# Mixer weight split in the first stage, h_in biases moved, second expert's low part inside slot 0

## The reference

```python
h = tok_embedding(x) * 16                     # tables of 256, 64, 16 and 4 columns, each projected to 256
n = layernorm(h)
x1 = n @ w1.T + w1_b
x_conv = silu(depthwise_conv3(x1))            # along the 128 positions
x_ssm = ssm(x_conv)                           # linear recurrence over positions, 16 states a channel
v = silu(n @ v1.T + v1_b)
h = h + (x_ssm * v) @ w2.T + w2_b             # the "mixer"
n = layernorm(h)
shared = (silu(n @ sw1 + sb1) * (n @ sw3 + sb3)) @ sw2 + sb2      # 512 hidden
out = (expert_a(n) + expert_b(n)) / 2         # 2 of 8 experts, each gelu(n @ w1 + b1) @ w2 + b2, 256 hidden
h = h + (shared + out) / 2
```

## Time and profile before

| | |
|---|---|
| median of three runs | 444.79 us (443.84 to 445.13) |
| profiled execution: its own time | 444.33 us |
| profiled execution: its span | 442.4 us, 8454 instructions |
| PE busy | 399.5 us (90%) |
| PEld (weight loads, beside PE) | 350.9 us (79%) |
| DVE busy | 281.8 us (64%) |
| ACT busy | 242.5 us (55%) |
| POOL busy | 213.1 us (48%) |

### The profile page before, as it was taken

The page is one execution under the profiler, slowest core; times in us unless marked ns, Lnnn a source line. Parts: engine busy times, 40 slices in busy tenths (PEclk is TensorE's granted clock), DMA queues, the critical chain, the costliest instruction groups (busy, mean ns, idle before and its releaser), DMA issues.

```text
span 442.4 us, 8454 instructions
## 1 busy us (share of the span) xinstructions
PE 399.5 (90%) x2880; PEld 350.9 (79%) x2880; DVE 281.8 (64%) x608; ACT 242.5 (55%) x435; POOL 213.1 (48%) x235
## 2 busy tenths in 40 slices
PE   3878899899998864799999999999999999998996
PEld 2767788888678762598898998988988988887885
DVE  6668998989655779866556465565554554655333
ACT  4675778778886335544544645635635635535442
POOL 7769998821008256547446337247247237333000
PEclk9999999999998989799999999999999999999999
DMA  2442121259799972100121021111201301100101
GB/s 63 122 148 95 43 66 52 73 166 305 220 309 282 254 273 84 50 0 3 54 90 46 31 68 48 53 42 47 80 15 48 92 3 48 47 0 0 49 0 47
DMA packets 32779, 38.86 MB, mean 88 GB/s; under 512 B 3461, under 2 KB 29027, under 8 KB 32624
## 3 DMA queue, kind: packets, MB, share of 16 engines
q1 hardware_dynamic: 29616, 32.99, 24.6%
...
...
## 4 chain that ended last, share of the span: by engine, by line
PE 67%; DVE 17%; ACT 6%; issue 4%; DMA 3%; POOL 1%; DVEq 0%; ACTq 0%; POOLq 0%; SPq 0%
PE ps L1139 20%; PE ps L1140 20%; PE ps L1141 20%; DVE hid_lo L1070 3%; DMA toep_l<-kernel_rows_dram 2%; DVE stat L948 2%; PE ps L1222 2%; PE ps L1177 2%; PE ps L1258 1%; DVE h2n L961 1%; DVE sw_lo L1017 1%; PE ps L1147 1%; DVE catT_lo L941 1%; DVE act_out L1064 1%; DVE hnT L990 1%
## 5 line engine op out<-in xcount | busy, mean ns | idle before, releaser
L1070 DVE SCALAR_TENSOR_TENSOR hid_lo<-act_out,hid_hi 128x512 fp32r<-128x512 f32 x64 | 56.2, 879 | 56.6 <-ACT hid_hi L855 56.6
L842 ACT ACTIVATE act_out<-ps,vec 128x512 f32<-128x512 f32 x32 | 22.1, 689 | 91.4 <-PE ps L1141 91.4
L1064 DVE SCALAR_TENSOR_TENSOR act_out<-ps,vec,act_out 128x512 f32<-128x512 f32 x32 | 24.0, 750 | 53.4 <-ACT act_out L842 53.4
L667 POOL TENSOR_TENSOR h_sb<-h_sb,bias_e 128x256 f32<-128x256 f32 x32 | 24.4, 766 | 53.4 <-DVE h2n L961 53.4
L1140 PE MATMUL ps<-h2nT_lo,sw_hi 128*128 128x512 f32 x128 | 50.0, 391 | 0.0
L1141 PE MATMUL ps<-h2nT_hi,sw_lo 128*128 128x512 f32 x128 | 50.0, 391 | 0.0
L1139 PE MATMUL ps<-h2nT_hi,sw_hi 128*128 128x512 f32 x128 | 49.9, 390 | 0.0
L660 POOL TENSOR_TENSOR zc_lo<-v_sb,zc_hi 128x256 fp32r<-128x256 f32 x32 | 29.6, 924 | 34.9 <-ACT zc_hi L832 34.9
L846 ACT ACTIVATE act_out<-ps,vec 128x512 f32<-128x512 f32 x32 | 22.1, 689 | 41.1 <-PE ps L1141 41.0
L527 POOL DMA_INDIRECT cat<-table_dram,x_ids x32 | 36.4, 1139 | 8.2 <-issue 5.8
L855 ACT ACTIVATE hid_hi<-act_out 128x512 fp32r<-128x512 f32 x64 | 39.7, 622 | 0.0
...
## 6 DMA issues: line engine op xcount, KB each, us to landing
...
```

Source lines behind the costliest of these rows:

```text
L667: nc.gpsimd.tensor_tensor(at, at, bias_e[:, bass.ds(e, 1), :].rearrange("p o c -> p (o c)"), ALU.add).then_inc(h2_biased, 1)
L842: nc.scalar.activation(act_out[:, n % 4, :], ps[bank][:, :], ACT.Silu, bias=vec[:, C_SB1 + j:C_SB1 + j + 1]).then_inc(act_done, 1)
L1064: nc.vector.scalar_tensor_tensor(act_out[:, n % 4, :], ps[bank + 1][:, :], vec[:, C_SB3 + j:C_SB3 + j + 1], act_out[:, n % 4, :], ALU.add, ...
L1070: nc.vector.scalar_tensor_tensor(hid_lo[:, n % 4, :], act_out[:, n % 4, :], 0.5 if kind == SHARED else 0.25, f32(hid_hi[:, n % 4, :]), ALU ...
```

## The change

Piece 0 gets a raw buffer of its own in the free end of `flat` (Toeplitz slot 3). It is loaded behind the first h store, cast by ScalarE behind the last hn of group 0, and its low part is formed by GpSimd at the start of the last group; SyncE waits for that low part before it loads Toeplitz slot 3. ScalarE's and VectorE's instructions for it between the recurrence and the mixer are gone, as are SyncE's load there and its wait ahead of piece 7. GpSimd adds the bias to both h_in buffers before piece_lo(1), and piece_lo(8) moves from ahead of slot 0 into mixer_1, behind its second mixer_bias.

```diff
--- before.py
+++ after.py
@@ -109,6 +109,7 @@
     power = flat[:, 0:HALVES * STATES * SEQ].rearrange("p (s t) -> p s t", t=SEQ)
     raw_at = HALVES * STATES * SEQ
     raw_a = flat[:, raw_at:raw_at + (KC + 4) * D]
+    raw_w2 = flat[:, raw_at + (KC + 5) * D:raw_at + (KC + 7) * D]
     k_sum = flat[:, raw_at + (KC + 4) * D:raw_at + (KC + 5) * D].rearrange("p (h t) -> p h t", t=SEQ)
 
 
@@ -387,13 +388,13 @@
 
 
     free = o_sb[:, :, :, :].rearrange("p a g c -> p (a g c)")
-    raws = [stage[:, 0, :], stage[:, 2:4, :], stage[:, 1, :]] + [free[:, n * BLK:(n + 1) * BLK] for n in range(4)]
+    raws = [raw_w2, stage[:, 2:4, :], stage[:, 1, :]] + [free[:, n * BLK:(n + 1) * BLK] for n in range(4)]
     raws += [stage[:, 0, :], stage[:, 2:4, :]]
     his = [w2_hi[:, :, :].rearrange("p k n -> p (k n)"), ex1_hi[:, :, :]] + [sw_hi[:, n, :] for n in range(6)]
     los = [w2_lo[:, :, :].rearrange("p k n -> p (k n)"), ex1_lo[:, :, :]] + [sw_lo[:, n, :] for n in range(6)]
     his, los = his + [ex0_hi[:, :, :]], los + [ex0_lo[:, :, :]]
     sources = [w_b[:, 0, :], w_e[RES - 1]] + [w_b[:, n, :] for n in range(1, 7)] + [w_e[0]]
-    LO_BY = (0, 1, 0, 0, 0, 0, 0, 0, 1)
+    LO_BY = (1, 1, 0, 0, 0, 0, 0, 0, 1)
     PIECES = [(raws[n], his[n], los[n], piece_sem[n], 16, LO_BY[n], LO_BY[:n + 1].count(LO_BY[n]), sources[n])
               for n in range(9)]
 
@@ -428,10 +429,15 @@
             toep_part(q, 0, HALF if q >= TRING else 0)
             toep_part(q, 1, 0)
 
+        def piece_in(n):
+            raw, _, _, signal, _, _, _, src = PIECES[n]
+            sp.dma_start(raw, src).then_inc(signal, 16)
+
         for r in range(RES):
             h_store(0, r)
             if r == 0:
                 sp.dma_start(raw_a[:, KC * D:], w_a[:, KC * D:]).then_inc(wa_in, 16)
+                piece_in(0)
         sp.dma_start(bias_row[:, 0:1, :], bass.AP(rows.tensor, D, [[0, P], [D, 1], [1, D]])).then_inc(rows_in, 16)
         sp.dma_start(bias_e[:, :, :], bass.AP(rows.tensor, 2 * D, [[0, P], [D, RES], [1, D]])).then_inc(rows_in, 16)
         with sp.Fori(1, GROUPS - 1) as i:
@@ -442,6 +448,8 @@
             if r == 1:
                 sp.wait_ge(k_out, 16)
                 sp.wait_ge(wv_lo_done, 2)
+            if r == 1 + TRIGHT:
+                sp.wait_ge(w_lo_done[1], 1)
             if 2 <= r < 2 + TRIGHT:
                 toep_load(r - 2)
 
@@ -464,10 +472,6 @@
             sp.dma_start(dst[bass.ds(r, 1), :, :, :].rearrange("o p g c -> (o p) g c"),
                          o_sb[:, par, :, :]).then_inc(stored[par], 16)
 
-        def piece_in(n):
-            raw, _, _, signal, _, _, _, src = PIECES[n]
-            sp.dma_start(raw, src).then_inc(signal, 16)
-
         def piece_used(n):
             sp.wait_ge(w_lo_done[PIECES[n][5]], PIECES[n][6])
 
@@ -476,15 +480,12 @@
         h_load(0, 0)
         sp.wait_ge(bias_step, BIAS_STEPS)
         sp.dma_start(w2_bias, bass.AP(rows.tensor, 0, [[0, P], [D, 1], [1, D]])).then_inc(rows_in, 16)
-        piece_in(0)
         piece_in(1)
         h_load(1, 1)
         piece_in(2)
         sp.wait_ge(ssm_done, 2 * NQ)
-        for n in range(3, 7):
+        for n in range(3, 8):
             piece_in(n)
-        piece_used(0)
-        piece_in(7)
         piece_used(1)
         piece_in(8)
         sp.wait_ge(h2_done, GROUPS)
@@ -590,9 +591,16 @@
                 pool.dma_start(kernel_rows, k_row[:, :, :, :].rearrange("p n c w -> p (n c w)").bitcast(F32)
                                ).then_inc(k_out, 16)
 
+        def piece_lo(n):
+            src, hi, lo, _, _, _, _, _ = PIECES[n]
+            pool.wait_ge(w_hi_done, n + 1)
+            nc.gpsimd.tensor_tensor(lo, src, f32(hi), ALU.subtract).then_inc(w_lo_done[1], 1)
+
         def group(i):
 
             for r in range(RES):
+                if i == GROUPS - 1 and r == 0:
+                    piece_lo(0)
                 if r % 2 == 0 and (r or i):
                     power_pair(RES * i + r - 2, (r - 2) % 4)
                 if r + LEAD < RES:
@@ -672,6 +680,7 @@
             for g in range(2):
                 mixer_lo(1, g)
                 mixer_bias(0, 0, g)
+            piece_lo(8)
             for g in range(GROUPS):
                 power_step(GROUPS + g, g, eps2_done, rstd2_done)
                 if g < 2:
@@ -710,20 +719,14 @@
             need(pool, l2_done, UNITS * e + 2, half_set)
             expert_split(e + 2, par, times)
 
-        def piece_lo(n):
-            src, hi, lo, _, _, _, _, _ = PIECES[n]
-            pool.wait_ge(w_hi_done, n + 1)
-            nc.gpsimd.tensor_tensor(lo, src, f32(hi), ALU.subtract).then_inc(w_lo_done[1], 1)
-
         pool.wait_ge(rows_in, 48)
         add_w2_bias(0, 1)
+        add_w2_bias(1, 1)
         piece_lo(1)
         for g in range(GROUPS):
             mixer_lo(0, g)
         for g in range(GROUPS):
             power_step(g, g, eps2_done, rstd2_done)
-        add_w2_bias(1, 1)
-        piece_lo(8)
         pool.wait_ge(w_lo_done[0], LO_BY.count(0))
         expert_in(2, 0)
         slot(0, 0, 2)
@@ -742,6 +745,11 @@
         nc.scalar.activation(warm_out[:, 0:1], zero[:, :], ACT.Silu)
         act.wait_ge(wa_in, 16)
         nc.scalar.copy(proj_hi[:, :, :].rearrange("p k n -> p (k n)"), raw_a[:, 0:KC * D]).then_inc(wa_hi, 1)
+
+        def piece_hi(n):
+            src, hi, _, signal, count, _, _, _ = PIECES[n]
+            act.wait_ge(signal, count)
+            nc.scalar.copy(hi, src).then_inc(w_hi_done, 1)
 
         def cat_hi(i, r):
             n = RES * i + r
@@ -767,6 +775,8 @@
             need(act, hn_turned, r // 2 - 1)
             nc.scalar.activation(hn[:, r % 4, :], h_ring[:, r % 4, :], ACT.Identity, bias=shift[:, r % 4:r % 4 + 1],
                                  scale=rstd[:, r % 4:r % 4 + 1]).then_inc(hn_first, 1)
+            if r == 7:
+                piece_hi(0)
             if r == 5:
                 act.wait_ge(wa_in, 32)
                 nc.scalar.copy(wv_hi[:, :, :, :].rearrange("p a k n -> p (a k n)"), raw_a[:, KC * D:]).then_inc(wa_hi, 1)
@@ -805,12 +815,6 @@
         act.wait_ge(pad_zero, 1)
         run_phase_a(act, {"cat": cat_hi, "emb": h_out, "norm": norm, "hn": hn_hi, "x": x_hi_part, "out": out_, "silu": silu})
 
-        def piece_hi(n):
-            src, hi, _, signal, count, _, _, _ = PIECES[n]
-            act.wait_ge(signal, count)
-            nc.scalar.copy(hi, src).then_inc(w_hi_done, 1)
-
-
         for q in range(NQ):
             if q == 1:
                 act.wait_ge(rows_in, 32)
@@ -820,7 +824,6 @@
             for bank in range(2):
                 act.wait_ge(ssm_done, 2 * q + bank + 1)
                 nc.scalar.copy(y_at(q, bank), y_part(q, bank, 1)).then_inc(y_low, 1)
-        piece_hi(0)
         act.wait_ge(ssm_done, 2 * NQ)
         piece_hi(1)
 
@@ -1102,8 +1105,6 @@
 
         for u in range(8, 16):
             z_part(u)
-            if u == 9:
-                piece_lo(0)
         for g in range(GROUPS):
             mixer_out(0, 0, g)
             if g >= 1:
@@ -1331,7 +1332,7 @@
         pe.wait_ge(y_done, 2 * NQ)
         for u in range(8, 16):
             y_turn(u)
-        pe.wait_ge(w_lo_done[0], 1)
+        pe.wait_ge(w_lo_done[1], 1)
         for g in range(GROUPS):
             mixer_mm(0, g)
         for g in range(GROUPS):
```

## The result

The changed kernel takes 441.38 us (median of 4 runs, 441.22 to 442.19) where the kernel before took 444.60 (443.84 to 445.13) beside it: ratio 0.9928, 95% interval 0.9904 to 0.9952. The forecast was 441.5.

The account below looks back on a forecast made before the run. The bound was when the near-continuous matmul stream from mixer_mm(1,0) starts, set by VectorE's sw_lo, GpSimd's DMA issue and tile 1's zc_lo. -4.0 + 0.75 + 0 = -3.25 against the 444.79 median gave 441.5 us, range 440.0 to 444.5.

Parts of the forecast that it names:

- signs named ahead: Signs of being right: short h2n and sw_lo, mixer_mm(1,0) about 3.3 us earlier, gap near 91 us, hid_lo under 1 us.
- sign of being wrong: First zc_lo chain ending after 169.5, TensorE idle before second(0,0), or first Toeplitz matmul over 1.3 us later.
- Phase A: Stage before the Toeplitz loads: GpSimd's early low part delays rstd, hn and catT_lo; TensorE loses about 0.75 us.
- my upper bound of 1.3: Upper bound for TensorE's loss from GpSimd's early low part; the lower was 0, the estimate 0.75 us.
- The rival of the late h_in: Second bias, ahead of every zc_lo, waits for late h_in; break-even at landing 163.3, at 165 446.5 us; slower, chance 0.08.
- The last norm: Tile 0's last normalization, with no bias beside it, ends at 174.0 instead of 176.36; hidden(0,0) 2.6 us earlier.
- step 2: Start of the mixer: without piece_lo(0) on VectorE, zc_lo ends at 168.4 against 168.72; gain 0.35, bounds -0.25 and +0.45.
- Four sw_lo: VectorE's low parts of shared weights, without piece_lo(8) beside them, take 2.45 us instead of 4.62: another 2.1 us.
- ScalarE is the late one now: Tile 1's zc_hi waits behind the first activation, clock low; mixer_mm(1,0) starts at 180.4 against 184.44: 4.0 us.
- piece_lo(8) in slot 0: GpSimd runs it behind zc_lo(1,1); norm(1,0) causes no wait, bounds 0 and +0.5; hid_lo gets in, cost 0.
- The rival that hid_lo is held: In slot 0, hid_lo is held behind piece_lo(8): 2.9 us come back, 444.4 us; chance 0.09.
- my bad case: Without GpSimd's gap in slot 0, hid_lo ends behind piece_lo(8) at 186.9: cost 2.9 us.

Follow-up runs that it names:

- after: The changed kernel itself, with all parts of the change: 441.38 us, ratio 0.9928 to the kernel before.
- e12: The changed kernel measured once more with no edit: 442.09 us, ratio 0.9942 to the kernel before.
- e6: Changed kernel plus matmuls whose results nobody reads, ahead of the mixer and around the transposes: 440.67 us, ratio 0.9909.
- e10: Changed kernel with the second h_in bias back behind the rstd steps: 441.82 us, ratio 0.9931.
- e8: Changed kernel with piece_lo(8) one place earlier in slot 0, right behind zc_lo(1,0): 442.58 us, ratio 0.9951.
- e2: Kernel before plus only the early mixer weight piece; second bias and piece_lo(8) stay where they were: 443.17 us, ratio 0.9955.
- e11: Changed kernel with low part at r = 3, second bias behind the rstd steps, unread matmuls only in the gaps of the turns: 439.83 us, ratio 0.9901.
- e5: Changed kernel with the low part of piece 0 three steps later in the last group, at r = 3: 441.63 us, ratio 0.9927.
- e7: Changed kernel with low part at r = 3 and unread matmuls in TensorE's gaps: 439.31 us, ratio 0.9880.
- e3: Kernel before with only the second h_in bias moved ahead of piece_lo(1): 445.0 us, ratio 0.9990.
- e1: Kernel before with the early second bias and piece_lo(8) in slot 0, without the early mixer weight: 442.78 us, ratio 0.9951.
- e9: Kernel before with the early second bias, and the first two mixer_bias of slot 0 moved behind the rstd step: 444.53 us, ratio 1.0004.
- e4: Kernel before with only piece_lo(8) moved into slot 0: 443.46 us, ratio 0.9961.
- part 1 alone: Kernel before plus only the mixer weight piece loaded, cast and split early: 443.17 us, ratio 0.9955.
- parts 1 and 3: Early mixer weight and piece_lo(8) in slot 0, second bias left behind the rstd steps: 441.82 us, ratio 0.9931.

## Why the prediction was right, step by step

Its time came out (441.5 against 441.38, then 442.09), and so did most of the path to it: where the clock stays low ahead of slot 0, where the two engines hold each other, what comes next. But that the first time was met to 0.1 us is luck. The forecast was a sum of -3.25 us; the stages of the two profiled executions give -2.6 and -2.8, and the second measured time is 2.2 us under before. One of the signs named ahead was missed: mixer_mm(1,0) starts 1.8 us earlier in the span (184.44 to 182.66) and not 3.3, 2.3 without the later start of that execution. And a sign of being wrong came up: the first Toeplitz matmul lies 1.6 us later in the span where the limit was 1.3, 0.5 of it the later start. Phase A cost 1.1 where 0.75 was said, the way from the first Toeplitz matmul to mixer_mm(1,0) gave 3.4 where 4.0 was said, and 0.3 came from behind second(0,0), where nothing was said.

1. Phase A was mis-sized: +0.75 was said, +1.1 measured, in after (98.13), e12 (98.03), e6 (98.00) and e10 (97.98); e8 lies at 97.90, and e2, at 98.85, above them. The mechanism is as said: rstd at 86.84, hn 1.20 late, catT_lo not ready, a gap of 0.47 at 91.65. What I left out is what follows the gap: TensorE's first hnT matmul starts 0.70 us behind the four transposes at 92.82 where it was 0.36 before, and VectorE's hnT, late itself, ends at 93.18. So the next turn of gathered rows moves from 93.38 to 95.02, 1.6 us later, of which 0.54 is there already at the turn before it. Between these two turns, near 91 and 95 us, it is 1.05 to 1.16 us more than before in all six kernels with the low part at its first place, and nothing in the other seven but one: e11, with its late rstd pair. e5 and e7 test it from the other side: with the low part at r = 3, A is 97.22 and 97.04, as before. What I passed on "in full" is not shown to arrive in full: see e5. ScalarE's cast costs nothing, as said: VectorE's step of 1.65 us beside GpSimd lasts 1.14 in after and ends where it ended, counted from the turn near 32 us. The loss between the two turns stays under my upper bound of 1.3 for the low part.

2. The early bias did not wait: h_in landed just as the first bias ended, and the two ran in 4.83 us without a gap. Counted from the first Toeplitz matmul it landed after 31.2 us instead of 31.8, the 0.6 that I had. But e3, with the removed DMA still in the queue, has 31.2 too, so no run shows that this DMA made the difference. Counted from the first Toeplitz matmul the last zc_lo ends 0.8 earlier (0.35 was said). But I looked at the last zc_lo alone. The first one is later, TensorE sits idle 2.27 us ahead of it, and the clock falls there, at about 167; the mixer's first matmuls run at 1.2 GHz. So B + C1 is 45.23 and 44.90 (after, e12) against 45.13: -0.1 to +0.2 gained at the last h2n where 0.35 was said. That fall of the clock was not foreseen. The rival of the late h_in had its place right: in e1, with the removed DMA in the queue, the second bias waited 0.75 us and B was 1.2 to 1.4 us longer than in the two executions of after. Break-even was at a wait of over 3 us.

3. The last norm: 0.41 us against 2.43, and C2 -2.28 where 2.25 (2.0 and 0.25 for the transposes) was said. e1, e3 and e9 show the same 1.8 with this edit, e2, e4 and e10 the 4.1 without. Forecast for hidden(0,0) was 2.6 with the 0.35 of step 2; from the first Toeplitz matmul it is 2.2 and 2.3 (47.05 in after, 46.97 in e12, 49.23 before).

4. Four sw_lo at 0.6 each against 4.62 us in all: as said, and e4 has the effect alone.

5. ScalarE is the late one now, as said: the first zc_lo of tile 1 waits 1.04 us for its zc_hi. The clock did fall again ahead of hidden(0,0), at about 177.1, and was back at 180.5; in e12 it fell at 174.8 and was back at 181.7, with the same C3. C3 went from 6.41 to 5.20 (5.0 was said). Counted from the first Toeplitz matmul, mixer_mm(1,0) starts at 52.25 instead of 55.64: 3.4 us, where 4.0 was said; most of the missing 0.6 is that of step 2. e6 priced what the fall costs: 1.0 us in C3, where I had 0.8.

6. piece_lo(8) in slot 0 costs nothing: hid_lo is in at 183.14 for 0.72 us, while GpSimd waits for zc_hi(1,1) as said (idle 0.47 us ahead of 183.78), and second(0,0) starts with no wait. The rival that hid_lo is held was tried in e8: put directly beside it, piece_lo(8) holds it for 2.25 us and TensorE still has what it needs. So this case costs nothing where I had 2.9 us. That hid_lo is held through the whole run of operations with piece_lo(8) at its end, which was my bad case, came up in no run. As for the rule of the Trainium skill (SBUF — State Buffer, Who interferes with whom), that the first to issue keeps the port pair for its whole instruction: e8 and e9 agree with it, where hid_lo waited for one GpSimd operation (2.25 us and 1.25 us); before (3.14 us) and e3 (3.25 us) do not, where it was held through three boundaries of four back-to-back operations. What decides at a boundary who is let in stays open: the four operations of e3 were zc_lo and bias in turn, the ones of e9 two zc_lo.

The parts don't add up one by one. By the medians, part 1 alone gives -2.0 us, the early bias -0.2, piece_lo(8) -1.75, together -4.0, with intervals of about 1.2 each way on each; the change gives -2.2 to -3.2. The bias alone loses its gain to the clock and to B (e3, e9). Part 1 trades about 1 us in phase A for a race: where piece_lo(0) loses it (before) the last h2n starts 45.1 us behind the first Toeplitz matmul, where it wins (e4) 43.0, as early as with part 1 alone (e2, 42.7) or with parts 1 and 3 (e10, 43.2). With part 1 in, the early bias takes from B what it gives in C2: 2.4 us of GpSimd's work stand ahead of zc_lo instead of ahead of the last norm (e10: B 34.84, C2 4.09; after: B 36.84, C2 1.82).
